# Two self-attention stages: half of the queries and keys projected ahead, the rest and the values between the first steps; the relative bias inside the attention block

## The chip, the cores and the metric

The kernel runs on one core of a Trainium2 chip. The metric is the device time of one execution in microseconds (us), the median of several runs. PE is TensorE (matmul), PEld its weight loads, DVE is VectorE, ACT is ScalarE, POOL is GpSimd, SP the engine whose queue issues the transfers.

## The reference, cut to what matters

The model takes x (16 sequences of 64 rows of 256 numbers, float32) through twelve sublayers; each normalises x and adds its own output to x. Two of the twelve are plain self-attentions over the 64 rows of a sequence, with 16 heads of 16 columns. L1_attn is the fifth sublayer, L3_attn the eleventh:

```python
def _L1_attn_ref(x, w_qkv, b_qkv, w_o, b_o):        # h = 16 heads, c = 16
    qkv = jnp.einsum('bld,ed->ble', x, w_qkv) + b_qkv
    q, k, v = jnp.split(qkv, 3, axis=-1)            # each reshaped to b, l, h, c
    attn = jax.nn.softmax(jnp.einsum('blhc,bmhc->bhlm', q, k) * SCALE, axis=-1)
    heads = jnp.einsum('bhlm,bmhc->blhc', attn, v).reshape(b, l, d)
    return jnp.einsum('bld,ed->ble', heads, w_o) + b_o + x

def _L3_attn_ref(x, W_attn, b_attn, W_proj, b_proj, rel_emb):
    qkv = x @ W_attn.T + b_attn                     # split into q, k, v, 16 heads
    rel_bias = rel_emb[buckets]                     # 64 x 64 positions, 32 buckets, 16 heads
    att = jnp.einsum('bhqd,bhkd->bhqk', q, k) * (1.0 / math.sqrt(D))
    att = att + rel_bias.transpose(2, 0, 1)[None]
    att = jax.nn.softmax(jnp.where(causal, att, -jnp.inf), axis=-1)
    y = jnp.einsum('bhqk,bhkd->bhqd', att, v)       # back to b, t, c
    return y @ W_proj.T + b_proj
```

The rows of `attn` and `att` sum to one. So the value bias adds the same row, bias of the values times the output weights, to every row of the result.

## The kernel before

The twelve sublayers run one after the other. Each is a chain of blocks; a block gives every engine its own list of instructions, and ends with a barrier of all engines (`signals`, line 44 of the profile), so nothing of a block starts before the one ahead of it has ended. An engine works through its list in order, and waits stand in the list.

Both self-attentions start with the block of `layernorm`. There SP issues the transfers of the stage's weights and waits for all of them, while DVE, ACT and PE normalise x and turn it into `h_T` (256 columns on two times 128 partitions, 1024 rows along the free axis).

`l3_attn` then has a block of its own for the relative bias. POOL clears `rel_bd` (line 4427), SP copies the 32 x 16 table of the bias into it four times (line 4433), PE multiplies it by the one-hot matrices of the buckets (line 4440, 16 matmuls of 64 columns), and DVE adds the causal mask while it puts the products into their place (line 4454, 16 instructions).

`self_attention` (line 1998) is one block in both sublayers:

- The projections. PE computes eight groups (line 2051), one for each of query or key, half of the 256 columns (m) and half of the 1024 rows (c); a group is two matmuls of 512 columns. ACT (lines 2145 and 2150) and DVE (lines 2190 and 2195) take the groups out of PSUM with the bias; a query group is written twice, with every other head zeroed. Then PE computes the values of eight tiles of 128 rows (line 2061, two matmuls of 256 columns each), and DVE takes them with their bias (line 2204, two instructions a tile).
- PE waits for all of these takes and goes into the steps: 14 of them, of which the first eight begin with the scores of a tile (line 2079, 32 small matmuls for two sequences).
- In step n DVE takes the scores of tile n. In L3_attn it first adds bias and mask (line 2225). It then finds the row maximum (line 2228) and subtracts it (line 2230), and after that sums the exponentials of tile n-1 (line 2240) and inverts the sums (line 2243). ACT computes the exponential (line 2159), POOL multiplies by the inverse (line 2042). PE turns the weights of tile n-3 (line 2092), ACT copies them out (line 2166), PE multiplies them by the values of tile n-4 (line 2107), ACT copies that (line 2173). The tile n-6 is multiplied by the output weights (line 2069, and line 2129 after the last scores), and DVE adds it to x (line 2214).
- POOL clears the place of the values (line 2030) and adds, to x, the normalised rows in L1_attn (line 2032) and the output bias in both (line 2035), ahead of its first multiplication.

The scores of a step overwrite those of the step before in the same PSUM banks, so PE waits in step n until DVE has read tile n-1: in L1_attn that is the end of the subtraction, in L3_attn the end of the bias addition, which is the first of the three:

```python
pe.wait_ge(act_taken, len(on_act))
pe.wait_ge(dve_taken, len(groups) - len(on_act))
pe.wait_ge(v_taken, T)
for n in range(T + OUT):
    if n >= 1:
        pe.wait_ge(shifted if bias is None else emptied, min(n, T))
```

Here T is 8 and OUT is 6. The turns of tile 0 come in step 3 (TURN), its product with the values in step 4 (WEIGHS).

## Time and profile before

| | us |
|---|---|
| runs of the kernel before | 3695.29, 3701.76, 3702.35 |
| their median | 3701.76 |
| the profiled execution, its time | 3699.78 |
| its span, from the first to the last instruction | 3697.9 |
| PE busy / DVE busy / ACT busy / POOL busy | 3387.1 / 2017.7 / 1689.2 / 702.9 |

The profiled execution took 1.9 us more than its span, and 2.0 us less than the median of the runs. Its mean granted TensorE clock was 0.954 of full speed. Times in the rows are counted from the first instruction of the span. L1_attn lies at 1819.5 to 1904.6 us: `layernorm` up to 1828.6, then `self_attention`. L3_attn lies at 3558.1 to 3665.7 us: `layernorm` up to 3569.7, the block of the relative bias up to 3585.1, then `self_attention`. Together they are 192.7 us, 5% of the span. In a row of the timeline the two first numbers are start and duration, "xN" the number of instructions that it merges, and the brackets hold how long the engine had been idle before it and which instruction ended that wait. A float32 matmul shows as two records on PE.

### The profile page before, as it was taken

To read this page: it belongs to the slowest core of one execution; us is meant where nothing else is said; L and a number is where in the kernel's file an instruction comes from. 1 tells how busy PE (TensorE), PEld (TensorE's weight loads), DVE (VectorE), ACT (ScalarE), POOL (GpSimd) and SP (SyncE) were. 2 spreads that over 40 slices of the span, in tenths; PEclk is the share of its full clock that TensorE was granted. 3 is DMA by queue.
4 is the path that set the end of the run, shared out by engine and by line. 5 is a ranking of instruction groups with operands and counts; after the bars stand their busy time and mean duration, and the time that the engine had idled before them with its cause. 6 is when DMAs were issued, how large, how long until landed. Compare 5 with 4: busy or idle time off the path is not lost. (4 is left out here: it accounts for less than half of the span.)

```text
span 3697.9 us, 90457 instructions
## 1 busy us (share of the span) xinstructions
PE 3387.1 (92%) x39440; PEld 2393.5 (65%) x39440; DVE 2017.7 (55%) x4041; ACT 1689.2 (46%) x3093; POOL 702.9 (19%) x344
## 2 busy tenths in 40 slices
PE   7999999799998989999879998999999789998975
PEld 4777777567765668888654455777776555554554
DVE  5667676744443367777556473655656433333337
ACT  4777777533332278787535452444444321111222
POOL 2767776311010000000122121101010000000001
PEclk9999999899998989999979999999999879999986
DMA  2111111111002316433010002111120013220710
GB/s 82 38 38 38 55 38 38 36 66 40 25 1 83 132 51 201 154 125 118 16 52 0 1 1 69 59 40 59 40 59 3 24 39 110 90 77 3 257 41 16
DMA packets 155268, 223.52 MB, mean 60 GB/s; under 512 B 39391, under 2 KB 134555, under 8 KB 154748
## 3 DMA queue, kind: packets, MB, share of 16 engines
q1 hardware_dynamic: 154876, 217.75, 17.8%
q8 instruction: 313, 5.13, 0.6%
q14 instruction: 79, 0.65, 0.1%
HBM read 216.67 MB, written 1.05 MB: 59 GB/s over the span
## 5 line engine op out<-in xcount | busy, mean ns | idle before, releaser
L3268 POOL TENSOR_TENSOR x_sc<-x_sc,h_T 128x2048 f32<-128x2048 f32 (+1 forms) x105 | 443.7, 4271 | 199.0 <-ACT h_T L3495 199.0
L3078 ACT ACTIVATE x_sc<-x_sc,x_nb 128x2048 f32<-128x2048 f32 (+1 forms) x112 | 210.6, 1880 | 297.7 <-DVE x_sc L3127 297.6
L3127 DVE SCALAR_TENSOR_TENSOR x_sc<-ps,x_nb,x_cap 128x2048 f32<-128x2048 f32 (+1 forms) x112 | 246.2, 2198 | 49.4 <-PE ps L3019 49.4
L3570 DVE TENSOR_TENSOR x_most<-x_most,ps 128x512 f32<-128x512 f32 (+1 forms) x352 | 234.9, 685 | 45.5 <-PE ps L3385 33.1
L1773 ACT ACTIVATE s1i_both<-ps,s_less,s_rs_s 128x64 f32<-128x64 f32 x624 | 214.8, 427 | 50.0 <-DVE s_less L1890 49.8
L3474 ACT COPY x_sc<-ps 128x1024 f32<-128x1024 f32 x192 | 179.3, 945 | 112.2 <-PE ps L3385 71.4
L3488 ACT ACTIVATE x_sc<-x_sc 128x2048 f32<-128x2048 f32 (+1 forms) x112 | 200.8, 1797 | 3.7 <-DVE x_sc L3268 3.7
L3341 PE MATMUL ps<-x_wv,x_ctx_T 128*128 128x256 f32 (+1 forms) x832 | 201.5, 384 | 0.0
L2990 PE MATMUL ps<-x_ctx_T,x_wk 128*128 128x401 f32 (+1 forms) x512 | 200.0, 518 | 1.5 <-PEq L44 1.5
L3333 PE MATMUL ps<-x_ctx_T,x_wk 128*128 128x401 f32 (+1 forms) x512 | 196.1, 521 | 5.4 <-POOL x_v L3297 3.8
L2998 PE MATMUL ps<-x_wv,x_ctx_T 128*128 128x256 f32 (+1 forms) x832 | 197.8, 379 | 0.0
L2998 PEld LDWEIGHTS ps<-x_wv,x_ctx_T 128*128 128x128 f32 (+1 forms) x832 | 154.7, 186 | 51.0 <-issue 3.4
L3111 DVE COPY x_v<-ps 128x512 f32<-128x512 f32 (+1 forms) x112 | 73.0, 652 | 208.3 <-PE ps L2998 208.3
L525 ACT ACTIVATE f_hid_T<-ps 128x512 f32<-128x512 f32 x68 | 40.6, 597 | 304.9 <-PE ps L488 304.9
L3341 PEld LDWEIGHTS ps<-x_wv,x_ctx_T 128*128 128x128 f32 (+1 forms) x832 | 150.8, 186 | 39.3 <-issue 3.0
L1667 PE MATMUL ps<-s_q,s1i_ctx_T 128*64 128x64 f32 x4992 | 159.0, 225 | 12.4 <-DVE s_q L1853 9.0
L1667 PEld LDWEIGHTS ps<-s_q,s1i_ctx_T 128*64 128x64 f32 x4992 | 154.8, 141 | 21.3 <-DVE s_q L1853 10.9
L1705 PE MATMUL ps<-s1i_ctx_n,s1i_both 128*64 128x257 f32 x1248 | 148.5, 388 | 8.2 <-DVE s1i_both L1910 8.2
L550 DVE SCALAR_TENSOR_TENSOR x<-ps,f_comb,x 128x256 f32<-128x256 f32 x192 | 84.0, 480 | 131.5 <-PE ps L503 131.5
L541 DVE TENSOR_TENSOR f_hid_T<-f_hid_T,ps 128x512 f32<-128x512 f32 x68 | 46.7, 687 | 192.6 <-PE ps L488 192.6
L2611 PE MATMUL ps<-g_ew,g_hm 128*128 128x512 f32 (+1 forms) x384 | 144.1, 530 | 0.0
L3333 PEld LDWEIGHTS ps<-x_ctx_T,x_wk 128*128 128x128 f32 x512 | 91.9, 192 | 68.3 <-POOL x_v L3297 4.7
(524 smaller groups left out, 6857.3 us busy)
## 6 DMA issues: line engine op xcount, KB each, us to landing
x_ctx_T<-in_ctx_T SPq DMA_DIRECT2D x32, 1601.0 KB
s1i_ctx_T<-in_ctx_T SPq DMA_DIRECT2D x16, 1601.0 KB, 7.9
x3i_ctx_T<-in_ctx_T SPq DMA_DIRECT2D x16, 1601.0 KB, 6.9
s1i_ctx_n<-in_ctx SPq DMA_DIRECT2D x16, 1536.0 KB
x3i_ctx_n<-in_ctx SPq DMA_DIRECT2D x16, 768.0 KB
h<-in_ctx SPq DMA_DIRECT2D x12, 896.0 KB
e_w<-in_L_attn_W SPq DMA_DIRECT2D x8, 1024.0 KB, 7.6
rows<-in_ctx SPq DMA_DIRECT2D x12, 640.0 KB
```

The source lines that it names most:

```text
L1667: last = nc.tensor.matmul(ps[side * S:(side + 1) * S, 2 * b + c, at:at + S], ctx_T[lane][:, b, k, keys], q2[lane][:, k, b * S:(b + 1) * S] ...
L1773: nc.scalar.activation(att[lane][:, b, t, :], ps[:, 2 * b + c, at:at + S], ACT.Exp, scale=rs_s[lane][:, b, t:t + 1], bias=less[lane][:, b, ...
L2990: last = nc.tensor.matmul(ps[:, bank, 0:width], w_k[:, k, m * P:(m + 1) * P], ctx_T[row % 2][:, k, at:at + width], start=(k == 0), stop=(k ...
L2998: last = nc.tensor.matmul(ps[0:keys, bank, j * D:(j + 1) * D], ctx_T[row % 2][:, k, t * P:t * P + keys], w_v[:, k, :], start=(k == 0), sto ...
L3078: nc.scalar.activation(x, x, ACT.Square, scale=DH ** -0.5, bias=nb[0:keys, 0:1]).then_inc(squared, 1)
L3127: nc.vector.scalar_tensor_tensor(out=slot[0:keys].rearrange("p r m h j q -> p (r m h) (j q)")[:, :, 0:width], in0=score_banks[0:keys].rear ...
L3268: return eng.tensor_tensor(x, x, most_of, ALU.subtract)
L3333: last = nc.tensor.matmul(ps[:, bank, 0:width], w_k[:, k, m * P:(m + 1) * P], ctx_T[row % 2][:, k, at:at + width], start=(k == 0), stop=(k ...
L3341: last = nc.tensor.matmul(ps[0:keys, bank, j * D:(j + 1) * D], ctx_T[row % 2][:, k, t * P:t * P + keys], w_v[:, k, :], start=(k == 0), sto ...
L3474: nc.scalar.copy(x[0:keys, rs].rearrange("p r h j q -> p r h (j q)")[:, :, :, 0:width], score_banks[0:keys, rs].rearrange("p r h j q -> p ...
L3488: nc.scalar.activation(x, x, ACT.Exp, scale=DH ** -0.5).then_inc(exped, 1)
L3570: ins = nc.vector.tensor_tensor(best[0:keys, rs], best[0:keys, rs], score_banks[0:keys, rs, :, j, :], ALU.max)
```

## The change

In `self_attention` the groups are ordered by half of the rows: groups 0 to 3 are query and key of the lower 512 rows, 4 to 7 of the upper ones. Only the first four are projected ahead of the steps. Two more follow the scores of step 0 and two those of step 1; the values of tiles 0 to 3 follow the scores of step 2, those of tiles 4 to 7 the scores of step 3. They use PSUM banks 4 to 7, two tiles of values to a bank. ACT takes groups 0, 2 and 4 to 7 and all the values, as plain copies between its exponentials; DVE takes groups 1 and 3.

The value bias is no longer added to the values. POOL spreads it over 128 columns (`bv_wide`), PE multiplies that by the output weights, DVE adds the product to the output bias (`b_ready`), and POOL adds the sum to x. PE waits for `b_ready` ahead of step 0, and POOL ahead of its addition.

In L3_attn the block of the relative bias is gone. Its matmuls stand ahead of the projections in the block of `self_attention`, its placing ahead of DVE's takes, and PE waits for the placing ahead of step 0. `rel_bd` is laid out with its zeros on the host and loaded by one transfer in `layernorm`, the first of seven; the row of the value bias (128 KB) is not loaded any more.

```diff
-def self_attention(nc, env, stage, w, b_col, b_rows, wo, scale, bias, also, sb):
+def self_attention(nc, env, stage, w, b_col, b_out, wo, scale, relative, also, sb):
...
+    bv_wide = sb("bv_wide", [P, KT, P])
...
-    groups = [(kind, m, c) for kind in "qk" for m in range(KT) for c in range(2)]
-    on_act = [0, 2, 4, 5, 6]
+    shared_at = ps[:, 2, NH - D:NH]
...
+    heads = [(kind, m) for kind in "qk" for m in range(KT)]
+    groups = [(kind, m, c) for c in range(2) for kind, m in heads]
+
+    def group_bank(g):
+        return 4 + g % 4
+
+    def value_bank(t):
+        return 4 + t // 2
...
+                nc.gpsimd.tensor_copy(
+                    bv_wide[:, :, :],
+                    b_col[:, 2 * KT:3 * KT].unsqueeze(2).broadcast_to([P, KT, P])
+                    ).then_inc(widened, 1)
                 nc.gpsimd.memset(v_par[:, :, :, :, :], 0.0).then_inc(cleared, 1)
                 if also is not None:
                     nc.gpsimd.tensor_tensor(env.x[:, :, :], env.x[:, :, :], also[:, :, :],
                                             ALU.add).then_inc(based, 1)
                     pool.wait_ge(based, 1)
+                pool.wait_ge(b_ready, 1)
...
+                def project_heads(g):
+                    kind, m, c = groups[g]
                     at = D * (kind == "k") + m * P
                     for k in range(KT):
-                        last = nc.tensor.matmul(ps[:, g, :], w[:, k, at:at + P],
+                        last = nc.tensor.matmul(ps[:, group_bank(g), :], w[:, k, at:at + P],
...
-                for t in range(T):
-                    if t in on_act:
-                        pe.wait_ge(act_taken, on_act.index(t) + 1)
-                    else:
-                        pe.wait_ge(dve_taken, t - sum(g < t for g in on_act) + 1)
...
+                def project_values(t):
+                        last = nc.tensor.matmul(
+                            ps[:, value_bank(t), t % 2 * D:(t % 2 + 1) * D],
+                            env.h_T[:, k, t * P:(t + 1) * P], w[:, k, 2 * D:3 * D],
...
+                def between(n):
+                    if n in (0, 1):
+                        project_heads(4 + 2 * n)
+                        project_heads(5 + 2 * n)
+                    elif n in (2, 3):
+                        for t in range(HALF * (n - 2), HALF * (n - 1)):
+                            if t % 2 == 0:
+                                pe.wait_ge(act_taken, 3 + value_bank(t) - 4)
+                            project_values(t)
...
-                    if n >= 1:
+                    if n == 0:
+                        pe.wait_ge(v_taken, 2)
+                    else:
...
-                    if n >= 1:
+                    if n == 0:
+                        pe.wait_ge(v_taken, 4)
+                    else:
...
-                pe.wait_ge(act_taken, len(on_act))
-                pe.wait_ge(dve_taken, len(groups) - len(on_act))
-                pe.wait_ge(v_taken, T)
+                if relative is not None:
+                    for g in range(S // 4):
+                        last = nc.tensor.matmul(ps[:, g // 8, (g % 8) * 4 * H:(g % 8 + 1) * 4 * H],
+                                                onehot[:, g, :], rel_bd[:, :, :], start=True,
+                                                stop=True)
+                    last.then_inc(tabled, 1)
+                for g in range(len(heads)):
+                    project_heads(g)
+                pe.wait_ge(widened, 1)
+                for k in range(KT):
+                    last = nc.tensor.matmul(shared_at, bv_wide[:, k, :], wo[:, k, :],
+                                            start=(k == 0), stop=(k == KT - 1))
+                last.then_inc(shared, 1)
+                if relative is not None:
+                    pe.wait_ge(placed, 16)
+                pe.wait_ge(act_taken, 2)
+                pe.wait_ge(dve_taken, 2)
+                pe.wait_ge(b_ready, 1)
                 for n in range(T + OUT):
+                    if n == HALF:
+                        pe.wait_ge(act_taken, 6)
...
+                        project(n - OUT).then_inc(s_done, 1)
+                    between(n)
...
-                act.wait_ge(bias_ready, 1)
-                for g in on_act:
+                def take_heads(g):
...
+                def take_values(pair):
+                    act.wait_ge(product, len(groups) + 2 * pair + 2)
+                    if pair == 0:
+                        act.wait_ge(cleared, 1)
+                    for j in range(2):
+                        ins = nc.scalar.copy(
...
+                    ins.then_inc(v_taken, 1)
+
+                act.wait_ge(bias_ready, 1)
+                take_heads(0)
+                take_heads(2)
                 for n in range(T + WEIGHS):
+                    if n < 2:
+                        take_heads(4 + 2 * n)
...
                         nc.scalar.activation(x, x, ACT.Exp, scale=scale).then_inc(exped, 1)
+                    if n < 2:
+                        take_heads(5 + 2 * n)
+                    elif n < HALF:
+                        take_values(2 * (n - 2))
+                        take_values(2 * (n - 2) + 1)
...
-                for g, (kind, m, c) in enumerate(groups):
-                    if g in on_act:
-                        continue
-                    dve.wait_ge(product, g + 1)
...
+                if relative is not None:
+                    dve.wait_ge(tabled, 1)
...
+                                nc.vector.scalar_tensor_tensor(
+                                    out=table[rows, :, at:at + 32],
...
+                                    op0=ALU.mult, op1=ALU.add).then_inc(placed, 1)
+                dve.wait_ge(product, 2)
+                for j in range(2):
+                    ins = nc.vector.tensor_scalar(
+                        q_bd[:, 1, 0:8, j, :],
+                        ps[:, group_bank(1), :].rearrange("p (b q) -> p b q", q=S),
+                        b_col[:, 1:2], env.parity[:, j:j + 1], ALU.add, ALU.mult)
+                    steps.done(ins) if j == 0 else ins.then_inc(dve_taken, 1)
+                dve.wait_ge(product, 4)
+                nc.vector.tensor_scalar(k_T[:, 1, 0:NH], ps[:, group_bank(3), :],
+                                        b_col[:, KT + 1:KT + 2], None, ALU.add
+                                        ).then_inc(dve_taken, 1)
+                dve.wait_ge(shared, 1)
+                nc.vector.tensor_tensor(b_out[:, :], b_out[:, :], shared_at, ALU.add
+                                        ).then_inc(b_ready, 1)
+                if relative is not None:
+                    dve.wait_ge(placed, 16)
...
         layernorm(nc, env, "a1_ln", env.x, env.h, env.h_T, loads=[
-            (w[:, :, :], wview(d["L1_attn_w_qkv"])), (wo[:, :, :], wview(d["L1_attn_w_o"])),
-            (b_col[:, :], d["L1_attn_b_qk"]),
-            (b_row[:, 0, :], d["L1_attn_b_qkv"][2 * D:3 * D].partition_broadcast(P)),
-            (b_row[:, 1, :], d["L1_attn_b_o"].partition_broadcast(P))])
-        self_attention(nc, env, "a1", w, b_col, b_row, wo, D ** -0.5, None, env.h, sb)
+            (w[:, :, :], wview(d["L1_attn_w_qkv"])), (b_col[:, :], d["L1_attn_b_qkv"]),
+            (wo[:, :, :], wview(d["L1_attn_w_o"])),
+            (b_out[:, :], d["L1_attn_b_o"].partition_broadcast(P))])
...
-            (w[:, :, :], wview(d["L3_attn_W_attn"])), (wo[:, :, :], wview(d["L3_attn_W_proj"])),
-            (b_col[:, :], d["L3_attn_b_qk"]),
-            (b_row[:, 0, :], d["L3_attn_b_attn"][2 * D:3 * D].partition_broadcast(P)),
-            (b_row[:, 1, :], d["L3_attn_b_proj"].partition_broadcast(P)),
-            (onehot[:, :, :], d["buckets"]), (causal[:, :], d["causal"])])
-
-        with signals(nc, "a3_bias", "zeroed table product placed") as (
-                zeroed, table, product, placed):
-            with nc.Block() as block:
...
-                    sp.wait_ge(zeroed, 1)
-                    for r in range(4):
-                        sp.dma_start(rel_bd[r * NB:(r + 1) * NB, r, :],
-                                     d["L3_attn_rel_emb"]).then_inc(table, 16)
...
+            (rel_bd[:, :, :], d["rel_bd"]), (onehot[:, :, :], d["buckets"]),
+            (causal[:, :], d["causal"]), (w[:, :, :], wview(d["L3_attn_W_attn"])),
+            (b_col[:, :], d["L3_attn_b_attn"]), (wo[:, :, :], wview(d["L3_attn_W_proj"])),
+            (b_out[:, :], d["L3_attn_b_proj"].partition_broadcast(P))])
+        self_attention(nc, env, "a3", w, b_col, b_out, wo, DH ** -0.5,
+                       (onehot, rel_bd, causal, table[:, :, :]), None, sb)
...
+    columns("L3_attn_b_attn")
+    a["rel_bd"] = np.zeros((P, 4, H), np.float32)
+    for r in range(4):
+        a["rel_bd"][32 * r:32 * r + 32, r] = a["L3_attn_rel_emb"]
```

## Rows read from the trace of the kernel before

**Rows 1.** Stretches of both attention stages: busy time (x count) of each engine, clock, DMA.

```profile
1828.60:1853.10 24.50, 23.78 (x64) 13.20 (x64) 7.88 (x22) 6.24 (x8) 12.50 (x3) 0.88 0.00 1
1853.10:1875.60 22.50, 13.78 (x240) 12.26 (x240) 16.81 (x17) 5.58 (x7) 5.70 (x3) 0.54 0.00 1
...
3569.60:3585.10 15.50, 7.09 (x32) 6.90 (x32) 3.42 (x16) 0.00 (x0) 0.15 (x1) 0.50 0.01 2
...
3608.60:3635.00 26.40, 15.23 (x278) 13.51 (x279) 24.32 (x24) 7.54 (x11) 6.99 (x4) 0.61 0.00 1
```

**Rows 2.** Timeline of the first stage (start, us, engine, instruction, [idle before]), its projections.

```profile
1828.70 16.87 PE L2051 MATMUL ps<-h_T,a_w 128*128 128x512 f32 x32 [1.79 <-PEq L44]
...
1835.31 1.53 DVE L2195 TENSOR_SCALAR a_q_bd<-ps,a_b_col,consts 128x512 f32<-128x512 f32 x2 [6.45 <-PE ps L2051]
...
1838.74 1.53 DVE L2195 TENSOR_SCALAR a_q_bd<-ps,a_b_col,consts 128x512 f32<-128x512 f32 x2 [1.90 <-PE ps L2051]
...
1844.60 1.28 ACT L2159 ACT_TABLE_LOAD   x1
...
1845.41 7.07 PE L2061 MATMUL ps<-a_w,h_T 128*128 128x256 f32 x32
...
1853.15 1.12 PE L2079 MATMUL ps<-a_k_T,a_q_bd 32*128 32x64 f32 x32 [0.67 <-DVE a_v_par L2204]
```

**Rows 3.** Timeline of the first stage, steps 0, 1 and 5.

```profile
1854.33 1.23 DVE L2228 TENSOR_REDUCE a_top<-ps 128x16 f32<-128x1024 f32 x1 [1.32 <-PE ps L2079]
...
1856.87 1.98 PE L2079 MATMUL ps<-a_k_T,a_q_bd 32*128 32x64 f32 x32 [2.60 <-DVE a_sc L2230]
...
1875.67 1.12 PE L2079 MATMUL ps<-a_k_T,a_q_bd 32*128 32x64 f32 x32
...
1876.85 1.23 DVE L2228 TENSOR_REDUCE a_top<-ps 128x16 f32<-128x1024 f32 x1 [0.27 <-PE ps L2079]
...
1877.37 1.06 PE L2092 MATMUL ps<-consts,a_sc 128*128 128x128 f32 x8 [0.58 <-ACT a_p_T L2166]
```

**Rows 4.** Groups by form, first stage (busy us, mean ns; idle before): its VectorE, ScalarE, GpSimd work.

```profile
L2230 DVE TENSOR_TENSOR a_sc<-ps,a_top 128x1024 f32<-128x1024 f32 x8 | 9.8, 1225 | 0.3
L2240 DVE TENSOR_REDUCE a_tot<-a_sc 128x16 f32<-128x1024 f32 x8 | 9.7, 1209 | 0.0
L2166 ACT COPY a_p_T<-ps 128x512 f32<-128x512 f32 x16 | 8.5, 582 | 2.6 <-PE ps L2092 2.6
L2159 ACT ACTIVATE a_sc<-a_sc 128x1024 f32<-128x1024 f32 x8 | 8.5, 1057 | 31.2 <-DVE a_sc L2230 31.2
...
L2035 POOL TENSOR_TENSOR x<-x,a_b_row 128x2048 f32<-128x2048 f32 x1 | 4.5, 4520 | 0.1
...
L2214 DVE TENSOR_TENSOR x<-x,ps 128x256 f32<-128x256 f32 x8 | 3.3, 411 | 9.0 <-PE ps L2129 9.0
```

**Rows 5.** Timeline of the last attention stage: the relative bias, the projections, the first scores.

```profile
3569.78 0.15 POOL L4427 MEMSET a_rel_bd<- 128x64 f32 x1 [166.16 <-POOLq L44]
...
3573.87 7.09 PE L4440 MATMUL ps<-a_rel_bd,a_onehot 128*128 128x64 f32 x32 [8.52 <-DMA a_rel_bd<-in_L_attn_rel_emb]
...
3585.19 15.86 PE L2051 MATMUL ps<-h_T,a_w 128*128 128x512 f32 x32 [4.22 <-PEq L44]
...
3594.22 1.53 DVE L2195 TENSOR_SCALAR a_q_bd<-ps,a_b_col,consts 128x512 f32<-128x512 f32 x2 [1.90 <-PE ps L2051]
...
3608.63 1.12 PE L2079 MATMUL ps<-a_k_T,a_q_bd 32*128 32x64 f32 x32 [0.67 <-DVE a_v_par L2204]
```

**Rows 6.** Stretches: the clock in both heads of the stages, the transfer ahead of the last.

```profile
1834.00:1835.00 1.00, 1.00 (x3) 0.48 (x2) 0.00 (x0) 0.00 (x0) 1.00 (x1) 0.73 0.00 0
3567.00:3568.00 1.00, 0.00 (x0) 0.00 (x0) 0.00 (x0) 0.00 (x0) 0.00 (x0) 1.00 0.35 137
3589.00:3590.00 1.00, 1.00 (x3) 0.44 (x3) 0.00 (x0) 0.96 (x2) 1.00 (x1) 1.00 0.00 0
```

**Rows 7.** Timeline of the last attention stage, step 5.

```profile
3634.03 1.23 DVE L2225 TENSOR_TENSOR a_sc<-ps,a_bias 128x1024 f32<-128x1024 f32 x1 [0.40 <-PE ps L2079]
```

125 lines of the change are left out of this document (40 added, 85 removed).

## The prediction

> **What bounds the kernel now.** I read the page first: PE is busy in 92% of the span, so a change here counts only by what leaves the chain of waits of its two stages. Every block ends with a barrier, so a microsecond taken out of a stage is one off the end, and nothing outside the two stages changes. Then the stretches of the stages [rows 1]: in the 24.5 us of projections of L1_attn PE is busy 23.8, DVE 7.9 and ACT 6.2, so PE alone sets them. In the first steps that turns round: PE has 13.8 of 22.5 us and a clock of 0.54 in L1_attn; in L3_attn DVE has 24.3 of 26.4 at 0.61. The block of the relative bias is 15.5 us in which PE works 7.1 and DVE 3.4, one after the other. The timelines say what ends the waits. The first scores start 24.45 us after the first projection, released by the last take of the values [rows 2]; scores 1 wait 2.6 us for the subtraction [rows 3]. So half of the projections and all values stand in a stretch that PE bounds, ahead of steps in which PE has room.
>
> **Part 1, the head of L1_attn.** The first half of the products is done when group 3 is: its take starts at 1838.74, 10.04 us after PE's start [rows 2]. Groups 4 to 7 and the values (the other 14.4 us) leave the head. Added on the path: the product of the value bias, four records of 256 columns at 7.07/32 = 0.22, so 0.9 us [rows 2]; DVE's addition for `b_ready`, 0.42 by the 0.411 of the same form [rows 4]; and a release, 0.14, as from DVE's last take to PE's scores before. DVE's take of group 3, one instruction of a pair's 1.53, runs beside that product. POOL's spreading of the bias is first needed 10 us in; it is hidden if it takes as much as the 4.5 us of the large addition [rows 4]. First scores: 1838.74 + 0.9 + 0.4 + 0.15 = 1840.2, against 1853.15. **Gain 12.95 us.**
>
> POOL now waits for `b_ready` ahead of its addition. Behind it on POOL stand only the multiplications, whose first input comes some 9.5 us after the first scores; the 4.5 us are over by then. Price nothing.
>
> **Part 2, the steps of L1_attn, counted from the first scores (T).** Scores take 1.12 us at full clock and 1.98 at half [rows 3]; two groups of projections are eight records of 512 columns, 3.43 us (the start of group 3's take is 3.43 behind that of group 1's) [rows 2]; four tiles of values 3.5. Maximum and subtraction are 1.23 each [rows 3, 4]. Before, the period was 1.98 + 0.1 + 2.5 = 4.6. After, PE itself sets it: scores 1 at T+4.65, scores 2 at T+9.2 (before T+8.3), scores 3 at T+13.9. Step 3 holds scores, values and the turn of tile 0 (1.06 [rows 3]): scores 4 at T+19.6, before T+17.5. Step 5 gives part back, because before it still ran at half clock: scores 5 at T+23.3, before 1875.67 - 1853.15 = T+22.5 [rows 2, 3], and DVE's maximum 5 at T+24.6 for T+23.7, behind its sums of tile 3 [rows 3]. **Loss 0.85 us.**
>
> ACT's new load hides. Its queue in step 0 is the take of group 4 (a pair like DVE's, 1.5), the table load (1.28, which before ran in the head with nothing behind it [rows 2]), exponential 0 (1.06 [rows 4]), take 5. Exponential 0 ends at T+6.7; DVE needs it at T+8.2. The values are eight copies of 256 columns, each under the 0.58 of a 512-column copy [rows 4]; I take 0.4, the end of the range nearest to it by columns, 3.1 us in all. The copy of tile 0 then ends at T+21.2, and PE's turn 1 waits 0.5 us for it beside DVE's maximum. At 0.58 each the turn comes 0.7 later, which is the bound.
>
> **Part 3, the block of the relative bias.** It goes with its POOL clear, four transfers, its barrier and 15.4 us (3569.78 to 3585.19) [rows 5]. Its PE and DVE work moves: 7.1 us of matmuls on PE's path, 3.45 us of placing that lies beside the projections and ends about when group 1 is there. The 4.1 us from POOL's clear to the first matmul (transfers) and the 4.3 from the last matmul to the first projection (placing, barrier) are what is saved. SP still issues seven transfers in `layernorm`; they, not the arithmetic, end that block, with DMA still at 0.35 in 3567 to 3568 [rows 6]. They are 96 KB fewer; at the 137 GB/s of that stretch this is 0.7 us at the most, while a small transfer now stands ahead of the large ones and may cost them as much. I take 0.3 gained, ends 0.7 lost and 0.7 gained.
>
> **Part 4, the head of L3_attn.** Start 3569.8 - 0.3 = 3569.5, relative bias to 3576.6. The projections start cold: group 3 took 9.03 us here [rows 5] and 10.04 in L1_attn [rows 2], because the clock rose about 3.8 and 5.6 us after their start [rows 6]. I take 9.5: 3586.1; plus 0.9, 0.4, 0.15 gives first scores at 3587.6 against 3608.63. **Gain 21.0 us.**
>
> **Part 5, the steps of L3_attn.** PE only waits for the bias addition, and DVE bounds: 3 x 1.23 + 1.21 [rows 4] and the small inversion, some 5.05 us a step. Once DVE is late it stays late: addition 1 at T+5.8 instead of T+4.8 (scores 1 stand behind two groups), addition 4 at T+21.0, and addition 5 at T+26.4, because scores 5 wait for the turn behind ACT's copies; before T+25.4 [rows 7]. **Loss 1.0 us.** POOL's addition now runs from T to T+4.4 beside DVE's subtraction 0, due at T+3.6. No row has such a pair; if it waits to the end, it is done at T+5.7, just when the next scores are, so this costs 0 to 0.1. The Trainium skill has that case: in "SBUF — State Buffer", section "Who interferes with whom", a VectorE instruction with two SBUF inputs and a GpSimd one that reads SBUF shut each other out for a whole instruction. By that rule the subtraction waits 0.8 us and the sum moves by 0.1 at most; without it, by nothing.
>
> **The sum.** 12.95 - 0.85 + 21.0 - 1.0 = 32.1 us. The profiled span would go from 3697.9 to 3665.8, its time from 3699.78 to 3667.7; the median stands 2.0 above that execution, so 3669.7. About 0.2%, 7.4 us, is what a measurement of this kernel can tell from no change.
>
> **The rivals.**
> - *PE's clock stays at half through the steps.* In the steps before, the mean fell to 0.54, and 13.8 us of work took 22.5 [rows 1]. If the new work ran at half speed, two groups would take 6.8 us and values 7: T comes 4.9 us later in each stage (13.65 us for four groups, 1.8 for the bias product), scores 4 at T+37.6. L1_attn then loses 20.1 in the steps and gains 8.1; L3_attn loses about as much, 20, and gains 16. Together 16 us slower, 3718. It decides from the point where about two thirds of these stretches run at half clock. Against it: PE was fed without a break in both heads and the clock rose each time [rows 6], and after the change it is busy for over 90% of each of the first four steps. Chance 2%. The Trainium skill, "TensorE: Matmul & The Clock Gate", section on the clock gate, calls the low clock the default and sustained activity what lifts it. By that rule the new steps stay at full clock; the heads agree, the relative bias's matmuls, 7.1 us at 0.50, do not.
> - *The clock falls for one or two of these steps*, at the wait for `b_ready` or at the turn of step 3: 5 to 14 us lost, 3675 to 3684, 8%.
> - *The clock is up sooner*, as the relative bias keeps PE busy right ahead of the projections in L3_attn: group 3 after 7.0 us instead of 9.5, and its steps 5 to 7 no longer at half clock, 1 us: 3666. For it: PE's rest ahead of them shrinks from 4.2 us to nothing [rows 5]. Against: 7.1 us of those matmuls did not lift it [rows 1]. 13%.
> - *ACT becomes the bound*, with values copies at 0.58 or more each and late turns: 2 us a stage, 3674, 5%.
> - That the change does not do what it says is excluded: PE's waits for groups 4 to 7 and for the values really stand behind the first scores.
>
> **How the numbers follow.** The forecast, 3669.7 us, has 72%. Its range: clock rise 1 us a stage, transfers 0.5, step prices 1.5 a stage, and 3 us for where the clock falls elsewhere, since the runs before lie 7 us apart. With the early clock and ACT's case that is 3662 to 3679, and it leaves out the two slow cases and the tails. Faster by over 0.2% (below 3694.4): all but the rival at half clock and a rest, 0.97. Within 0.2%: 0.01. Slower: 0.02.
>
> **What would show it.** Right: first scores 11.5 us after the first projection in L1_attn and about 18 us after the block's start in L3_attn; starts of scores 0 to 4 4.6, 4.6, 4.7 and 5.7 apart; a clock of 1.0 throughout; later steps as before. Wrong: records of 512 columns of 0.85 us between the scores, DVE waiting for ACT's exponentials, or the first matmul of L3_attn's block after 3570.5.

## The result and the profile after

The changed kernel took 3660.74 us (median of four runs, 3657.97 to 3662.27), the kernel before, beside it on the same chip, 3700.47: a ratio of 0.9892, 95% interval 0.9879 to 0.9904. The forecast was 3669.7 us, its range 3662 to 3679, so this median lies 1.3 us below the range. Two more series of the same kernel, run beside experiments, gave 3667.15 and 3670.16. Over all its 15 runs the median is 3666.0 (3657.97 to 3675.67), and over the 36 runs of the kernel before it is 3701.8 (3694.5 to 3711.1). So the change is worth 35.8 us, where 32.1 were forecast; the first four runs stood at the low end.

The page of the changed kernel, part 1:

```profile
span 3660.1 us, 90440 instructions
## 1 busy us (share of the span) xinstructions
PE 3377.9 (92%) x39448; PEld 2376.7 (65%) x39448; DVE 2007.4 (55%) x4007; ACT 1696.5 (46%) x3113; POOL 703.4 (19%) x345
```

PE is still busy in 92%. As little work went away, the gain is work that moved under other work. Its timeline in L1_attn, PE's queue and what releases it (to be read beside [rows 2, 3]):

```profile
1829.14 7.11 PE L2067 MATMUL ps<-h_T,a_w 128*128 128x512 f32 x16 [1.79 <-PEq L44]
...
1836.09 1.03 PE L2153 MATMUL ps<-a_wo,a_bv_wide 128*128 128x256 f32 x4
...
1836.29 0.75 DVE L2273 TENSOR_SCALAR a_k_T<-ps,a_b_col 128x512 f32<-128x512 f32 x1 [1.90 <-PE ps L2067]
1837.15 0.42 DVE L2277 TENSOR_TENSOR a_b_out<-a_b_out,ps 128x256 f32<-128x256 f32 x1
...
1837.72 1.12 PE L2104 MATMUL ps<-a_k_T,a_q_bd 32*128 32x64 f32 x32 [0.60 <-DVE a_b_out L2277]
...
1838.77 3.70 PE L2067 MATMUL ps<-h_T,a_w 128*128 128x512 f32 x8
...
1842.26 1.28 ACT L2218 ACT_TABLE_LOAD   x1
1842.40 1.12 PE L2104 MATMUL ps<-a_k_T,a_q_bd 32*128 32x64 f32 x32
...
1851.75 1.18 ACT L2203 COPY a_v_par<-ps 128x256 f32<-128x256 f32 x4
```

The first scores start 8.58 us after the first projection (24.45 before), and DVE's `b_ready` releases them. Scores 1 have no wait in brackets: eight projections stood ahead of them, so PE itself sets the step.

The stretches of the head and of steps 0 to 3 in L1_attn, then the relative bias and steps 0 to 4 in L3_attn (columns as in [rows 1]):

```profile
1829.10:1837.70 8.60, 7.97 (x20) 3.73 (x21) 3.09 (x5) 2.13 (x3) 8.32 (x3) 1.00 0.01 2
1837.70:1857.30 19.60, 19.58 (x184) 13.67 (x184) 13.94 (x14) 11.19 (x19) 8.67 (x4) 1.00 0.01 2
3553.80:3560.10 6.30, 6.30 (x33) 6.30 (x33) 0.38 (x1) 0.00 (x0) 3.83 (x2) 0.55 0.01 3
3570.90:3597.30 26.40, 23.66 (x320) 17.19 (x320) 24.33 (x24) 14.31 (x24) 10.45 (x5) 1.00 0.01 2
```

The second row is the change in one line: 19.58 of 19.60 us busy, clock at full. Before, a stretch of these steps had PE busy for 13.78 of 22.5 at 0.54 [rows 1]. In L3_attn DVE works the same 24.3 of 26.4 us as before, while PE does 8.4 us more there (23.66 against 15.23).

The timeline of L3_attn's head (beside [rows 5, 6]):

```profile
3553.80 6.49 PE L2145 MATMUL ps<-a_rel_bd,a_onehot 128*128 128x64 f32 x32 [2.36 <-PEq L44]
...
3560.09 9.36 PE L2067 MATMUL ps<-h_T,a_w 128*128 128x512 f32 x16
3560.33 3.45 DVE L2257 SCALAR_TENSOR_TENSOR a_table<-ps,a_causal 64x128 f32<-64x128 f32 x16 [6.15 <-PE ps L2145]
...
3570.85 4.53 POOL L2050 TENSOR_TENSOR x<-x,a_b_out 128x2048 f32<-128x2048 f32 x1 [13.23 <-DVE a_b_out L2277]
...
3570.92 1.12 PE L2104 MATMUL ps<-a_k_T,a_q_bd 32*128 32x64 f32 x32 [0.61 <-DVE a_b_out L2277]
...
3574.69 1.78 DVE L2301 TENSOR_TENSOR a_sc<-a_sc,a_top 128x1024 f32<-128x1024 f32 x1
```

The clock differs from one profiled execution to the next where the code is the same, so three of each kernel are laid side by side below. The layernorm is counted from its table load, the head from the first projection to the first scores, and the steps from there to the next stage's table load (us; means of three, single ones in brackets where they differ by over 0.5):

| piece | before | after | gain | forecast |
|---|---|---|---|---|
| L1 layernorm | 9.14 | 9.04 | 0.1 | 0 |
| L1 head | 23.19 (24.45, 23.55, 21.56) | 8.57 | 14.6 | 12.95 |
| L1 steps | 51.73 (51.44, 50.82, 52.92) | 52.51 | -0.8 | -0.85 |
| L3 layernorm to POOL's clear / to the first matmul | 11.59 | 9.63 | 2.0 | 0.3 |
| L3 bias block / bias matmuls to the first projection | 15.67 | 6.34 | 9.3 | 8.3 |
| L3 head | 23.40 | 10.78 | 12.6 | 12.5 |
| L3 steps | 57.06 | 58.20 (57.23, 57.23, 60.13) | -1.1 | -1.0 |
| both stages | 191.8 | 155.1 | 36.7 | 32.1 |

The code between the two stages is unchanged, yet took 1654.2, 1657.8 and 1663.7 us in three profiles of the changed kernel, and 1653.5, 1653.2 and 1657.4 in those of the kernel before. So the spans of the six profiles differ by 32.1 us in the mean, although the stages gained 36.7; the medians of all runs lie between, at 35.8. Differences of a few us between runs are therefore read in the stages, not in the whole time.

The steps of L3_attn show what a single execution can carry. The first four steps are alike in all profiles. Of the stretch from 24 to 41.5 us after the first scores, the first row is from the first profile of the changed kernel (steps of 57.23 us), the second from the third (60.13). The granted clock was full in the one and 0.70 in the other:

```profile
3594.92:3612.42 17.50, 11.62 (x385) 9.62 (x385) 16.29 (x19) 7.49 (x16) 5.71 (x3) 1.00 0.01 3
3602.35:3619.85 17.50, 15.11 (x320) 12.78 (x320) 13.98 (x16) 7.05 (x15) 5.70 (x3) 0.70 0.01 2
```

### The profile page after: what moved, and what is told of

The parts are those of the page before. It is cut to its first block and busy times, and to the rows that moved or that the text cites. A ratio compares the mean times of both kernels' runs of the same rounds, so it can differ in the third digit from the quotient of the medians.

```text
span 3660.1 us, 90440 instructions
## 1 busy us (share of the span) xinstructions
PE 3377.9 (92%) x39448; PEld 2376.7 (65%) x39448; DVE 2007.4 (55%) x4007; ACT 1696.5 (46%) x3113; POOL 703.4 (19%) x345
```

## The experiments

All are edits of the changed kernel; "the changed kernel" means its three profiles of the table. Where two programs are compared by medians, the changed kernel stands at 3666.0.

**1. The order alone.** All projections and values go back ahead of the steps; the value bias product and the relative bias stay as changed.

```diff
                 for g in range(len(heads)):
                     project_heads(g)
+                for g in range(len(heads), len(groups)):
+                    pe.wait_ge(act_taken if g % 2 == 0 else dve_taken, (g - 4) // 2 + 1)
+                    project_heads(g)
+                for t in range(T):
+                    if t % 2 == 0:
+                        pe.wait_ge(act_taken, 3 + value_bank(t) - 4)
+                    project_values(t)
...
-                    between(n)
```

> All eight groups and the values of all eight tiles are projected ahead of step 0 again, with the changed kernel's banks and takes; nothing stands between the steps. Theory A (PE's order is what gained in both stages): the first scores come 16 x 0.43 + 32 x 0.22 = 13.9 us later in each stage, and the steps get back some 1 to 2 us a stage (scores 4 at T+17.5 instead of T+19.6 in L1_attn). That is 24 to 26 us slower than the changed kernel, about 3685, with steps 1 to 3 of L1_attn at a half clock again. Rival B (most of the gain is the full clock in the steps, not the order): if PE stays at full clock in the steps here too, they shrink by 0.9 us each and the loss is under 22 us, about 3681.

Measured: 3689.88 us (8 runs), ratio 0.9971 (0.9959 to 0.9982). The changed kernel is 24 us faster by medians; by the stages it is 29.2 (184.3 against 155.1). The timeline of L1_attn, and the stretches of head and steps:

```profile
1827.80 15.90 PE L2067 MATMUL ps<-h_T,a_w 128*128 128x512 f32 x32 [1.79 <-PEq L44]
...
1852.08 1.12 PE L2104 MATMUL ps<-a_k_T,a_q_bd 32*128 32x64 f32 x32 [0.61 <-DVE a_b_out L2278]
...
1855.80 1.98 PE L2104 MATMUL ps<-a_k_T,a_q_bd 32*128 32x64 f32 x32 [2.60 <-DVE a_sc L2302]
```

```profile
1827.80:1852.00 24.20, 23.67 (x68) 13.61 (x68) 3.09 (x5) 9.67 (x18) 8.31 (x3) 0.92 0.01 1
1852.10:1874.70 22.60, 13.93 (x243) 12.24 (x243) 16.98 (x17) 6.25 (x8) 10.19 (x4) 0.58 0.01 1
```

The old picture is back: PE waits 2.6 us for the subtraction, the clock of the steps is 0.58, the same scores take 1.98 us instead of 1.12. Rival B, a full clock here too, did not come. The interleaving carries most of the gain, in both stages (first scores 15.7 us later in L1_attn, 12.8 in L3_attn).

**2. The block of the relative bias alone.** Its four transfers, POOL's clear and its barrier come back, and the transfer of the zero-filled `rel_bd` goes; the rest stays.

```diff
-                if relative is not None:
-                    for g in range(S // 4):
-                        last = nc.tensor.matmul(ps[:, g // 8, (g % 8) * 4 * H:(g % 8 + 1) * 4 * H],
...
-            (rel_bd[:, :, :], d["rel_bd"]), (onehot[:, :, :], d["buckets"]),
+            (onehot[:, :, :], d["buckets"]),
...
+        with signals(nc, "a3_bias", "zeroed landed product placed") as (
+                zeroed, landed, product, placed):
+            with nc.Block() as block:
```

> The relative bias is back in a block of its own, with POOL's clear and four small transfers; the rest is the changed kernel. Theory A: the block costs 15.4 us again and takes 6.3 to 7.1 us of matmuls out of the next one, so 8.5 to 9 us slower, about 3669.5; PE then starts the projections after a rest of 4.2 us. Rival B (the matmuls of the relative bias warm the clock for the projections, and that is part of the gain): 1 to 3 us more, 3671 to 3673, with group 3 later than 9.4 us after the first projection.

Measured: 3676.17 us (4 runs), ratio 0.9925 (0.9901 to 0.9948), 10.2 above the changed kernel. Timeline of L3_attn:

```profile
3559.61 0.15 POOL L4468 MEMSET a_rel_bd<- 128x64 f32 x1 [166.15 <-POOLq L44]
...
3563.69 7.09 PE L4481 MATMUL ps<-a_rel_bd,a_onehot 128*128 128x64 f32 x32 [5.89 <-DMA a_rel_bd<-in_L_attn_rel_emb]
...
3575.00 8.62 PE L2067 MATMUL ps<-h_T,a_w 128*128 128x512 f32 x16 [4.22 <-PEq L44]
```

From the clear to the first projection it is 15.39 us again, and 24.45 from the table load; in the changed kernel's first profile that is 15.70. That is the block, 8.75, as expected. Rival B did not come: the first scores start 10.09 us after the first projection, no later than in the changed kernel (10.83, 10.83 and 10.68). The steps took 60.75 us here against 57.23, 57.23 and 60.13, with the same code and the first four starts equal to 0.01; the clock was 0.81 from 24 to 41.5 us after the first scores, where the first profile of the changed kernel had 1.00, so that part of the difference is the clock and not the block. The head of L1_attn, which this edit does not touch, took 1.7 us more as well. That is why the median lies above the 3669.5 that was expected.

**3 and 4. Why the layernorm of L3_attn became shorter.** In e3_old_order the seven transfers are issued in the old order (large weights first, then the columns and rows); e4_old_order_row also loads the row of 128 KB again.

```diff
-            (rel_bd[:, :, :], d["rel_bd"]), (onehot[:, :, :], d["buckets"]),
-            (causal[:, :], d["causal"]), (w[:, :, :], wview(d["L3_attn_W_attn"])),
-            (b_col[:, :], d["L3_attn_b_attn"]), (wo[:, :, :], wview(d["L3_attn_W_proj"])),
-            (b_out[:, :], d["L3_attn_b_proj"].partition_broadcast(P))])
+            (w[:, :, :], wview(d["L3_attn_W_attn"])), (wo[:, :, :], wview(d["L3_attn_W_proj"])),
+            (b_col[:, :], d["L3_attn_b_attn"]),
+            (b_out[:, :], d["L3_attn_b_proj"].partition_broadcast(P)),
+            (rel_bd[:, :, :], d["rel_bd"]), (onehot[:, :, :], d["buckets"]),
+            (causal[:, :], d["causal"])])
```

> The transfers of L3_attn's layernorm in the order of before (weights first, the two tables of the relative bias last), without the row of the value bias. In the changed kernel the block lasts 9.4 us, before 11.7. Theory A (the order gained it: the 128 KB row spread to all partitions and the small columns no longer stand among the large transfers): 11 us or more. Rival B (the missing row gained it): 9.4 to 9.9.

> As the run before it, and one more transfer of a 128 KB row spread over the partitions, where the value bias was; it is not used. Theory A (order): about as the run before it, 11 to 12 us. Rival B (the row): 2 us longer than the run before it, 11.7. Both runs also show when the clock rises in the head of L1_attn, whose code is that of the changed kernel: if it is chance, the first scores come anywhere from 8.6 to 11.5 us after the first projection; if the change brings it, always 8.6.

Measured from the table load to the first matmul: 11.87 us in e3_old_order and 12.54 in e4_old_order_row, against 9.41, 9.59 and 9.90. By these runs 2.0 to 2.5 us are the order and 0.7 a row. The order can be told from the scatter: of eleven profiles with the changed kernel's order nine have 9.39 to 9.91 us; in the other two, 11.19 (e7_warm) and 10.57 (e11_best2), SP took 1.52 and 1.40 us to issue the transfer of the large weights instead of 0.43. The row's 0.7 is the difference of two single profiles, and the kernel before, with the row but without the transfer of `rel_bd`, took 11.59, less than e3_old_order without it; so that figure is not firm. The times, one run of each, 3660.74 and 3669.24 us, say nothing at this size. The stretches of the changed kernel, the last two columns the DMA share and GB/s:

```profile
3547.00:3548.00 1.00, 0.33 (x2) 0.29 (x2) 0.97 (x3) 0.98 (x2) 0.00 (x0) 0.50 1.03 418
...
3551.00:3552.00 1.00, 0.44 (x4) 0.20 (x2) 0.54 (x2) 0.59 (x1) 0.00 (x0) 0.99 1.06 353
3552.00:3553.00 1.00, 0.00 (x0) 0.00 (x0) 0.17 (x1) 0.00 (x0) 0.00 (x0) 1.00 0.29 98
```

and of e3_old_order, whose stage begins at 3539.30 (the changed kernel's at 3544.39):

```profile
3543.00:3544.00 1.00, 1.00 (x6) 0.58 (x4) 0.53 (x6) 1.00 (x4) 0.00 (x0) 0.50 0.93 280
3544.00:3545.00 1.00, 1.00 (x6) 0.75 (x5) 1.00 (x4) 0.44 (x2) 0.00 (x0) 0.50 0.43 59
...
3549.00:3550.00 1.00, 0.00 (x0) 0.00 (x0) 0.00 (x0) 0.00 (x0) 0.00 (x0) 1.00 0.08 29
```

In the kernel before, whose stage begins at 3558.13, the rate falls in the same way:

```profile
3561.00:3562.00 1.00, 0.58 (x3) 0.38 (x4) 0.96 (x7) 1.00 (x3) 0.00 (x0) 0.50 1.01 397
...
3563.00:3564.00 1.00, 1.00 (x6) 0.92 (x6) 1.00 (x4) 0.43 (x2) 0.00 (x0) 0.50 0.70 134
```

In the old order the large weights come first, then the columns and rows, then the tables of the relative bias. There the rate falls to 59 GB/s for a microsecond in mid-transfer and the last transfer ends some 10 us after the stage's start. In the changed kernel the rate stays at 353 to 424 GB/s and all is in some 8 us after. Its columns, too, stand between the two large weights, so which transfer lowers the rate was not taken apart.

**5. POOL's addition beside DVE.** POOL's addition waits for the subtraction of step 0 as well, so that it meets step 1's.

```diff
                 pool.wait_ge(b_ready, 1)
+                pool.wait_ge(shifted, 1)
```

> POOL adds the output bias to x only when the subtraction of step 0 is done. In L3_attn of the changed kernel that subtraction lasted 1.78 us instead of 1.23, and ended 1.1 us after POOL's addition. Theory A (VectorE's subtraction with two inputs in SBUF and POOL's addition shut each other out): subtraction 0 is 1.23 again, and subtraction 1, which now meets POOL's addition in its last microsecond, is longer, about 2.3 us, so that everything behind it in L3_attn comes up to 1 us later; in L1_attn, where the subtraction reads its scores from PSUM, nothing changes. Rival B (something else stretched subtraction 0, PE's or ACT's traffic): it stays at 1.78 and subtraction 1 at 1.22.

Measured: 3660.39 us (one run). Timeline of L3_attn, steps 0 and 1:

```profile
3567.85 1.22 DVE L2302 TENSOR_TENSOR a_sc<-a_sc,a_top 128x1024 f32<-128x1024 f32 x1
3569.23 4.53 POOL L2051 TENSOR_TENSOR x<-x,a_b_out 128x2048 f32<-128x2048 f32 x1 [16.75 <-DVE a_sc L2302]
3569.96 1.23 DVE L2297 TENSOR_TENSOR a_sc<-ps,a_table 128x1024 f32<-128x1024 f32 x1 [0.88 <-PE ps L2105]
3571.22 1.22 DVE L2300 TENSOR_REDUCE a_top<-a_sc 128x16 f32<-128x1024 f32 x1
3572.47 2.37 DVE L2302 TENSOR_TENSOR a_sc<-a_sc,a_top 128x1024 f32<-128x1024 f32 x1
```

The subtraction with both inputs in SBUF takes 1.22 us alone and 2.37 beside POOL's addition: it ends 1.08 us after that addition, so it did next to nothing until POOL was done. The bias addition (one input in PSUM) and the maximum, both wholly inside the addition, keep 1.23 and 1.22. In the changed kernel subtraction 0 met the addition's tail, 1.78 us (above), and PE's scores 1 (3575.60) had not ended by then, so it cost nothing. Here it costs: DVE's additions 2 to 4 come 1.14 us later after the first scores than in the changed kernel, against the up to 1 us expected. The steps as a whole took 62.3 us, part of it because the clock fell ahead of step 5; the run's time, low even so, does not show it. The Trainium skill, "SBUF — State Buffer", section "Who interferes with whom", has this rule for two SBUF inputs; the trace agrees, and its price here is the rest of POOL's instruction.

**6. The wait for `b_ready`.** The value bias product moves to bank 4, and PE waits for `b_ready` behind the first scores.

```diff
-    shared_at = ps[:, 2, NH - D:NH]
+    shared_at = ps[:, 4, 0:D]
...
+                pe.wait_ge(act_taken, 1)
...
-                pe.wait_ge(b_ready, 1)
...
                 def between(n):
+                    if n == 0:
+                        pe.wait_ge(b_ready, 1)
```

> The product of the value bias goes to bank 4 and PE waits for b_ready only after the scores of step 0. Theory A: the first scores start right after DVE's take of group 3, 0.55 us sooner in each stage (8.05 instead of 8.6 us after the first projection where the clock is full). Rival B: DVE's addition of the bias then delays the first maximum and nothing is gained at the second scores, since PE's own work sets the steps: T+4.68 stays, so the whole stage is 0.5 sooner anyway; if DVE sets it, the gain is gone by step 2.

Measured: 3667.64 us (one run). Timeline of L1_attn:

```profile
1844.51 1.03 PE L2156 MATMUL ps<-a_wo,a_bv_wide 128*128 128x256 f32 x4
1844.71 0.75 DVE L2275 TENSOR_SCALAR a_k_T<-ps,a_b_col 128x512 f32<-128x512 f32 x1 [1.90 <-PE ps L2067]
1845.58 0.42 DVE L2279 TENSOR_TENSOR a_b_out<-a_b_out,ps 128x256 f32<-128x256 f32 x1
1845.61 1.12 PE L2106 MATMUL ps<-a_k_T,a_q_bd 32*128 32x64 f32 x32
```

The scores start 0.90 us behind the start of DVE's take of group 3, against 1.43 in the changed kernel (1836.29 to 1837.72). The wait is worth 0.53 us a stage, as the prediction's 0.42 plus 0.14 had it; the product itself (1.03) remains on the path. The whole head took 10.81 us all the same, because the clock rose only 5.6 us after the first projection (1834.80).

**7. Is the early clock in L1_attn's head the layernorm's doing?** Three matmuls on constants are put into the layernorm blocks of both stages, two ahead of the turns and one behind.

```diff
+                def keep_warm(count):
+                    for _ in range(count if stage in ("a1_ln", "a3_ln") else 0):
+                        nc.tensor.matmul(env.ps[:, 7, :], env.ident, env.consts[:, 0:NH],
+                                         start=True, stop=True)
+
+                keep_warm(2)
...
+                keep_warm(1)
```

> In the two layernorm blocks ahead of the self-attentions PE also does two matmuls of 512 columns on constants before its transposes and one after them, whose results are not used. Theory A (the head of L1_attn costs 8.6 to 11.3 us only because the clock sometimes rises late): the first scores come 8.6 us after the first projection or a little less. Rival B (the rise is chance whatever PE did before): anything up to 11.5. In L3_attn the 64-column matmuls of the relative bias still run at half clock, so the head stays at 16.5 to 17.5 us in all.

Measured: 3673.02 us (one run). The stretches of the changed kernel ahead of L1_attn's projections, then of e7_warm:

```profile
1826.00:1827.00 1.00, 1.00 (x7) 0.95 (x5) 0.64 (x2) 0.05 (x1) 0.00 (x0) 0.50 0.00 0
1827.00:1828.00 1.00, 0.35 (x2) 0.00 (x0) 0.61 (x1) 0.59 (x1) 0.00 (x0) 0.86 0.00 0
```

```profile
1826.00:1827.00 1.00, 0.76 (x7) 0.57 (x6) 0.96 (x4) 0.58 (x2) 0.00 (x0) 1.00 0.32 111
1827.00:1828.00 1.00, 1.00 (x8) 0.72 (x7) 1.00 (x4) 0.44 (x2) 0.00 (x0) 1.00 0.00 0
```

In the changed kernel the clock rose from 1.2 to 2.4 GHz as the turns of the layernorm's rows ended, ahead of the first projection; in the first profile of the kernel before it rose some 5.8 us into the projections (0.73 over 1834 to 1835 [rows 6]). But in the third profile of the kernel before (e14_before_third, first projection at 1827.96) it was up in time as well, and the head was 21.56:

```profile
1827.00:1828.00 1.00, 0.04 (x1) 0.07 (x1) 0.03 (x1) 0.00 (x0) 0.08 (x1) 1.00 0.00 0
```

So an early clock does not need the change. With the extra matmuls the turns themselves run at 1.00 and the layernorm takes 8.43 us instead of 9.13, but the steps behind took 53.88 for 52.51, and the stage as a whole 70.9 for 70.0 to 70.2. The head is 8.57, as in the changed kernel's three profiles. But the same head, with no edit to it or to the blocks before it, took 10.28 us in e2_bias_block and 11.34 in e4_old_order_row, and 8.58 in e3_old_order; e5_pool_late, whose edit of POOL's wait lies behind the first scores, had 11.49, and e6_no_b_ready 10.81. So without the extra matmuls an execution may have it either way: five of nine profiles of the new head have the clock up in time. All four programs with them (e7, e11, e12, e15) have it, one profile each; that fits Theory A, but four are too few to exclude chance. In L3_attn nothing came of it: 3.8 us without PE work pass there while the transfers end, and the relative bias starts cold again (6.85 us).

**8. The relative bias between the projections.** Its matmuls go in two halves behind groups 0 and 1.

```diff
                 for g in range(len(heads)):
                     project_heads(g)
+                    if relative is not None and g < 2:
+                        for i in range(8 * g, 8 * g + 8):
+                            last = nc.tensor.matmul(
+                                ps[:, g, (i % 8) * 4 * H:(i % 8 + 1) * 4 * H],
+                                onehot[:, i, :], rel_bd[:, :, :], start=True, stop=True)
+                        last.then_inc(tabled, 1)
```

> In L3_attn the matmuls of the relative bias stand in two halves behind groups 0 and 1 instead of ahead of all groups, and DVE places them half by half. Theory A (the 64-column matmuls let the clock fall, and a group after them starts cold): the clock stays full or rises within the head, which takes 11 to 14 us from the first matmul to the first scores instead of 17.1. Rival B (the matmuls cost what they cost and the clock rises at a time of its own): 16 to 17 us.

Measured: 3659.73 us (one run). Timeline of L3_attn:

```profile
3551.63 3.08 PE L2067 MATMUL ps<-h_T,a_w 128*128 128x512 f32 x4 [2.58 <-PEq L44]
...
3554.51 2.48 PE L2147 MATMUL ps<-a_rel_bd,a_onehot 128*128 128x64 f32 x16
...
3558.60 1.89 PE L2147 MATMUL ps<-a_rel_bd,a_onehot 128*128 128x64 f32 x16
```

The second half runs at full clock: 16 records in 1.89 us, 0.118 each, where [rows 5] have 7.09 us for 32, 0.222 each. From the first matmul to the first scores it is 13.82 us against 17.1 in the changed kernel, but its steps took 60.15, so the stage's total, 83.88, is that of the changed kernel's best profile (83.76). Better in the head; whether in the run, one run can't say.

**9 and 10, 13 and 14. Both kernels again**, beside the versions below. These are the second and third profiles of the table.

> The changed kernel once more, unaltered, with more rounds. Theory A (of the gain beyond the forecast some 2 us are the order of the transfers, and the rest is where the clock happened to rise): the median comes at 3660 to 3665, 37 to 40 us under the kernel before; the head of L1_attn anywhere between 8.6 and 11.5 us, the steps of L3_attn 57 to 61. Rival B (the early clock belongs to the change): head 8.6 and steps 57.2 again, 3660 or less.

> The kernel before once more, for a second profile. Theory A (chance of the clock): its head in L1_attn, 24.45 us in the first profile with a rise 5.8 us after the first projection, may come down to 21.5 to 24.5, and the steps of L3_attn, 57.1, go anywhere to 60; the block of L3_attn's layernorm 11.7 again, since its transfers are the same. Rival B: all of them the same within 0.3 us.

> The changed kernel a third time. So far its median was 3660.7 us in one series and 3667.2 in the next, while both profiles gave the two attention stages the same time (70.2 and 83.8 to 83.9 us). Theory A (the stages gain 38.5 us by themselves less what the clock takes by chance in the heads, and the two series differ by the rest of the kernel): a median of 3660 to 3668; the two stages together 154 us if the clock rises early in L1_attn, up to 157 if it rises late. Rival B (the gain of the first series was the stages' own and the second series was a slower chip): 3660 again within 2 us.

> The kernel before a third time, for its profile. Theory A: L1_attn 83 to 85 us, L3_attn 107.6 within 1 us. Rival B (its first two profiles were lucky or unlucky in the clock): outside that.

Measured: the changed kernel 3667.15 us (5 runs, ratio 0.9904, 0.9888 to 0.9921) and 3670.16 (6 runs, 0.9909, 0.9893 to 0.9925); the kernel before 3697.05 and 3701.81 (one run each as a kernel of its own, with 9 and 11 runs beside it at 3702.14 and 3702.55). Three intervals of the same comparison overlap, and two of the three medians of the changed kernel lie inside the forecast's range. Both repeated medians lie above what was expected of them (3660 to 3665 and 3660 to 3668). The heads of L1_attn in the kernel before (23.55 and 21.56) and its L3_attn (107.6 and 107.9) came as expected.

**11, 12 and 15. Versions to beat the changed kernel.** e11_best2 has experiments 6, 7 and 8 together. In e12_best_all the matmuls on constants stand in every later layernorm block that turns rows, too (nine blocks; the expectations count eight). e15_warm_only has these matmuls alone, without 6 and 8.

```diff
+                ahead, behind = (2, 2) if stage == "a3_ln" else (2, 1) if first is None and dst_T is not None else (0, 0)
```

> The changed kernel with three edits: the relative bias in halves behind groups 0 and 1 (2.5 us in the run with that alone), PE's wait for b_ready behind the first scores (0.53 us a stage), and PE kept busy on constants in the two layernorm blocks (2 matmuls ahead; 1 and 2 behind). Theory A: 4 to 7 us under the changed kernel, 3654 to 3660; the head of L1_attn 8.05 us, that of L3_attn 11 to 13.5 us from the first matmul. Rival B (the clock of the later steps takes it back): within 2 us of the changed kernel.

> As the run before it, and the matmuls on constants in every layernorm block that turns its rows (six more). Theory A (each following block starts its matmuls at a full clock and would lose up to 1.5 us else): 2 to 8 us under the run before it. Rival B (the other stages warm up in their own time and hardly depend on it, or the extra matmuls end later than the block did): the same within 3 us.

> The changed kernel with nothing but the matmuls on constants in the eight layernorm blocks that turn their rows. The kernel with these and the two other edits had 3650.5 us, with them in two blocks only 3664.7. Theory A (the kept clock in the other stages made the difference): 3650 to 3657. Rival B (the mixed order in L3_attn and the later wait made it, and chance hid it in the other run): 3660 to 3668.

Measured: 3664.70 us (5 runs, ratio 0.9893, 0.9877 to 0.9909), 3650.52 (4 runs, 0.9854, 0.9839 to 0.9869) and 3657.93 (5 runs, 0.9872, 0.9854 to 0.9889). e12_best_all beats both kernels: 51 us under the kernel before, 15 under the changed one, with an interval that stands clear of the changed kernel's. e11_best2 can't be told from the changed kernel, which is its Rival B. e15_warm_only lies 8 us under the 3666.0, and 12 under the series of the changed kernel beside it (3670.16, 0.9893 to 0.9925), whose interval it just clears; that of the first series (0.9879 to 0.9904) it overlaps. It falls between its two theories. The groups by line that show what the matmuls on constants do, first the changed kernel, then e12_best_all:

```profile
L182 PE MATMUL ps<-consts,h 128*128 128x128 f32 x160 | 39.9, 429 | 60.8 <-ACT h L163 60.8
```

```profile
L180 PE MATMUL ps<-consts 128*128 128x512 f32 x56 | 35.0, 745 | 21.8 <-PEq L44 20.0 <-DVEq L44 1.7
L191 PE MATMUL ps<-consts,h 128*128 128x128 f32 x160 | 30.9, 331 | 18.8 <-ACT h L163 18.2
```

The turns of rows in all these blocks take 9.0 us less (39.9 to 30.9), for 35 us of added work, most of it in time in which PE only waited. Not all: in the block that starts at 3355.39 in the changed kernel PE's next work comes 9.54 us after the table load for 8.83, behind the added matmuls. How much of the 15 us is the turns, how much the head of L3_attn (first matmul to first scores 11.61 us for 17.1) and how much the blocks that follow was not taken apart. The profiled execution of e12_best_all, 3661.92, is its slowest run: its span, 3660.0, is no shorter than that of the changed kernel's first profile (3660.1), and its two stages together, 152.2, are 2.9 us under the mean of the table. So no trace here shows where the 15 us lie.

## Why the prediction came out 1.3 us outside its range

**Part 1, L1_attn's head: the mechanism right, one term mis-sized.** Product, addition and release were 1.03, 0.42 and 0.15 for 0.9, 0.4 and 0.15, and POOL's spreading of the bias (0.40 us) is hidden. The step that failed is "its take starts at 1838.74, 10.04 us after PE's start": in the changed kernel it is 7.15. The 10.04 is the row of one execution, in which the clock rose late; the kernel before itself had a head of 21.56 in another. The prediction allowed 1 us a stage for the rise, and by the three profiles it is 2.9 between two executions of the same kernel. Against the means of three the term is 1.7 us short. That the three profiles of the changed kernel all have 8.57 is chance as far as is known: four other programs with the same head had 10.28 to 11.49.

**Part 2, the steps of L1_attn: right.** Scores 1 to 5 start 4.68, 9.36, 14.06, 19.63 and 23.36 us after scores 0, for 4.65, 9.2, 13.9, 19.6 and 23.3. The loss is 0.8 for 0.85. ACT hides its table load and copies four times in 1.18 us, 0.3 each, for the 0.4 taken.

**Part 3, the transfers: the second term mis-sized.** "I take 0.3 gained, ends 0.7 lost and 0.7 gained"; measured 2.0. Only the bytes were priced (0.7; experiment 4 has 0.67 for a row, by one run). Their new order was in the diff and was bounded by one small transfer, while a sign of its price was in the trace: in the kernel before the rate falls from 397 to 134 GB/s between 3561 and 3564. Experiment 3 shows that the order alone is 2.0 to 2.5 us. The block of the relative bias is a third, smaller term, 9.3 for 8.3: its matmuls to the first projection took 6.3 us for 7.1, as the clock was partly up at the start (0.55 over them, by the third stretch above), and the block before lasted 15.7 in the mean of three for the 15.4 of one.

**Part 4 and 5, L3_attn: right.** First scores 10.8 us after the first projection for 10.95. Addition 1 comes at T+5.87 (forecast 5.8), addition 5 at T+25.96, and at 26.95 in the third profile (26.4); the steps lose 1.1 for 1.0. The meeting with POOL's addition costs DVE 0.55 us in subtraction 0 and the sum nothing, inside the 0 to 0.1 given.

**The rivals.** The half clock in the steps (2%) did not come: scores 1 to 4 start at the same places, within 0.01 us, in every profile of the new order. So the clock did not fall for one or two of these steps either (8%), nor was ACT the bound. Of the signs given for "right", the four distances (4.68, 4.68, 4.70 and 5.57 us) and the clock of 1.0 came; the head of L1_attn, 11.5 us, did not. The clock that is up sooner (3666, 13%) gave the time that all runs have, but by luck and not where it was put: it came up early in L1_attn, out of the layernorm, where the prediction looked for it behind the relative bias in L3_attn. The 7 us spread of the runs before was taken for the kernel's; over 36 runs it is 17.

**In sum**: 36.7 us in the stages for 32.1; 1.7 of the difference is the head of L1_attn, 1.7 the transfers, 1.0 the relative bias. Taken off the 3701.8 of the kernel before, that gives 3665, inside the range. The first four runs stood 9.0 us under the forecast: 5.5 are in the profiled execution (3662.18 for 3667.7), and 3.4 in the step "the median stands 2.0 above that execution", which took one execution's place among its runs for a constant: in these four the median stood 1.4 below it. That profile had the stages only 1.1 us under their mean, and the unchanged code between them 4.4; the other three runs have no trace, so where they were fast stays open.

## What to carry to other kernels

A head that PE bounds and steps in which it waits are one reserve: work moved from the first to the second pays twice, because it also keeps the clock up where it used to fall (1.00 for 0.54 in the first steps of L1_attn). Before taking a duration at a stage's start from one execution, look at the granted clock there; it may be that execution's alone. The order of transfers in a queue is an edit with a price of its own: read the rate in each microsecond of the block before.

## What the runs showed of the hardware

- TensorE busy throughout does not by itself bring the higher clock: 32 records of 64 columns, back to back, ran at 0.50 and 0.55 for over 6 us; in the second case the clock fell within the first microsecond of them, from 1.00. The same instructions behind projections of 512 columns ran at full clock, 1.89 us for 16.
- The time at which the clock rises differs between executions of the same code: one head took 8.57, 10.28 and 11.34 us in programs that are alike up to its end, the head of the kernel before 21.56, 23.55 and 24.45, and the steps of L3_attn 57.2 and 60.1.
- The order of seven transfers in one queue was worth 2.0 to 2.5 us: with the columns and rows behind the large weights and ahead of the tables the rate fell to 59 GB/s for a microsecond; with the tables first and the row last it stayed at 353 to 424. Which transfer lowers it is open.
- A VectorE subtraction with both inputs in SBUF made next to no progress beside a GpSimd addition until that ended: 2.37 us for 1.22, ending 1.08 us after it. A bias addition with one input in PSUM kept its 1.23.
